# Attention stage of a four-layer graph network: row numbers of two steps in one load and one comparison, a ring of 18 steps for the gathered rows, the block's maximum in other forms

## The reference

```python
def _L3_gnn_ref(x, edge_index, edge_attr, W, w_att, bias):
    h = x @ W
    src, dst = (edge_index[0], edge_index[1])
    x_i = h[dst]
    x_j = h[src]
    wa = w_att[0]
    alpha = x_i @ wa[:c] + edge_attr @ wa[c:c + ce] + x_j @ wa[c + ce:]
    alpha = jnp.where(alpha > 0, alpha, NEG_SLOPE * alpha)      # 0.2
    m = jax.ops.segment_max(alpha, dst, num_segments=n)
    m = jnp.where(jnp.isfinite(m), m, 0.0)
    a = jnp.exp(alpha - m[dst])
    s = jax.ops.segment_sum(a, dst, num_segments=n)
    a = a / (s[dst] + 1e-16)
    out = jax.ops.segment_sum(a[:, None] * x_j, dst, num_segments=n) + bias
    return out
...
x = _layernorm(x + _L3_gnn_ref(x, edge_index, edge_attr_16, L3_gnn_W, L3_gnn_w_att, L3_gnn_bias), axis=-1)
```

## Time and profile before

| what | value |
|---|---|
| median of 3 runs | 3815.82 us (3812.74 to 3816.24) |
| profiled execution | 3803.94 us, span 3802.2 us |
| VectorE busy over the span | 3118.7 us (82%) |
| TensorE busy | 3011.9 us (79%) |
| ScalarE busy | 2164.2 us (57%) |
| GpSimd busy | 1355.7 us (36%) |
| HBM traffic | 237 GB/s over the span |
| attention stage | from about 2855 us to the end |

### The profile page before, as it was taken

How to read it: one execution, slowest core, us unless ns; L and a number is a source line. 1 busy time by engine, 2 the same in 40 slices (tenths; PEclk the granted TensorE clock), 3 DMA queues, 4 the chain that set the end, 5 groups by cost and what they waited for, 6 DMA issues and landing times.

```text
span 3802.2 us, 124955 instructions
## 1 busy us (share of the span) xinstructions
PE 3011.9 (79%) x50473; PEld 2686.6 (71%) x50473; DVE 3118.7 (82%) x6534; ACT 2164.2 (57%) x5758; POOL 1355.7 (36%) x1644
## 2 busy tenths in 40 slices
PE   0288888888888869999778777787776888888786
PEld 0177777777777759899677777777766777777775
DVE  7599999999999933223599999999977889888996
ACT  5323333333333320000388888888866888888887
POOL 2000000000000000000088887887883555555554
PEclk9999999999999989999899999999986878888887
DMA  8156666666666689898687777777747888888884
GB/s 216 55 157 207 207 208 208 209 210 209 207 210 208 214 284 380 344 339 323 232 269 239 253 250 242 250 256 232 247 157 248 265 260 272 269 270 260 270 270 141
DMA packets 655934, 907.61 MB, mean 239 GB/s; under 512 B 363977, under 2 KB 587882, under 8 KB 636411
## 3 DMA queue, kind: packets, MB, share of 16 engines
q1 hardware_dynamic: 633240, 800.64, 65.5%
q10 hardware_dynamic: 19763, 94.38, 6.5%
q0 software_dynamic: 2352, 4.52, 0.6%
HBM read 651.96 MB, written 247.40 MB: 237 GB/s over the span
## 4 chain that ended last, share of the span: by engine, by line
DVE 37%; PE 31%; DMA 9%; issue 8%; ACT 7%; SPq 2%; POOL 1%; ACTq 0%; DVEq 0%; POOLq 0%
PE ps L630 7%; PE ps L976 7%; DVE U L758 5%; DMA U<-AD 3%; DVE A L1292 3%; DVE EDG L781 3%; DVE EDG L1316 3%; DMA A<-ROWS 3%; DMA T<-ROWS 3%; DVE U L1284 3%; PE ps L1199 2%; DVE U L1666 2%; DVE EDG L1671 2%; ACT U L546 2%; PE ps L1211 2%
## 5 line engine op out<-in xcount | busy, mean ns | idle before, releaser
L546 ACT ACTIVATE U<-ps 128x512 bf16<-128x512 f32 (+1 forms) x637 | 359.1, 573 | 666.0 <-PE ps L642 664.5
L1169 POOL TENSOR_TENSOR EDG<-U,edge 128x256 f32<-128x256 f32 x343 | 244.1, 712 | 780.4 <-DVE edge L1312 678.6
L1491 ACT ACTIVATE U<-U,T 128x65 f32<-128x65 f32 x1806 | 459.7, 340 | 76.4 <-PE ps L1582 65.5
L491 POOL DMA_INDIRECT U<-REC,nod x49 | 45.0, 918 | 1163.5 <-PE ps L586 1042.5
L976 PE MATMUL ps<-U 128*128 128x192 bf16 x4802 | 416.9, 248 | 30.8 <-DMA U<-AD 30.5
L1199 PE MATMUL ps<-U 128*128 128x65 bf16 x7203 | 296.8, 198 | 173.4 <-DVE A L1292 171.5
L976 PEld LDWEIGHTS ps<-U 128*128 128x128 bf16 x4802 | 401.9, 98 | 39.3 <-DMA U<-AD 35.9
L781 DVE TENSOR_TENSOR EDG<-edge,EDG 128x896 bf16<-128x896 bf16 x686 | 407.8, 620 | 10.0 <-DMA OSD<-EDG 9.1
L1199 PEld LDWEIGHTS ps<-U 128*128 128x128 bf16 x7203 | 258.0, 100 | 195.8 <-DVE A L1292 191.0
L1519 POOL TENSOR_TENSOR U<-U 128x455 f32<-128x455 f32 x258 | 275.8, 1069 | 296.2 <-DVE U L1666 296.2
L655 PE MATMUL ps<-EDG,U 128*128 128x193 bf16 x2401 | 312.9, 252 | 62.3 <-ACT U L546 40.8
(11 more groups left out here) (299 smaller groups left out, 7148.5 us busy)
## 6 DMA issues: line engine op xcount, KB each, us to landing
U<-AD SPq DMA_DIRECT2D x98, 1568.0 KB, 8.5
U<-ROWS SPq DMA_DIRECT2D x343, 448.0 KB, 4.6
OND<-EDG SPq DMA_DIRECT2D x343, 224.0 KB, 2.3
OSD<-EDG SPq DMA_DIRECT2D x343, 224.0 KB, 3.1
AD<-U ACTq DMA_DIRECT2D x49, 1568.0 KB, 6.4
EDG<-ROWS SPq DMA_DIRECT2D x343, 224.0 KB, 5.0
U<-OND SPq DMA_DIRECT2D x303, 224.0 KB, 5.2
EDG<-OSD SPq DMA_DIRECT2D x189, 224.0 KB, 4.8
```

The costliest lines, as they stand in the source:

```text
L546: ev4.by(act.activation(prow[i % NPW][:, P * g:P * (g + m)], ps[4 + gg % 2][:, 0:P * m], ACT.Copy))
L1491: ins = act.activation(V4[k % NV][:, 0, c, :], H[d % 3][:, s, :], ACT.Copy, scale=a4[d % 2][:, s:s + 1])
```

## The change

Row numbers. ROWS3 is laid out with the source rows of all blocks first and the target rows after them, so that two steps stand next to each other also across blocks. `sources(u)` and `targets(u)` load the row numbers of steps 2u and 2u + 1 at once (448 KB, 128 x 1792), and VectorE compares them at once. There are NU4 = 172 such pairs in place of 343 steps, 5 slots of double size for each kind, in other places of SBUF. SyncE issues the sources of pair t // 2 + 4 at even t; VectorE compares the sources of pair t // 2 + 2 at even t, and the targets of pair u at t = 2u + 7. The targets of a pair are issued at t = 2u + 4, or later when TensorE has not yet reached L1572's place for the block whose steps occupied the slot (`freed`).

Ring. `H` is a ring of 18 steps, where it was 21 (three blocks). Where a block goes over the end of the ring, alpha and the setting of the column are made in two pieces. The preparation uses a view `Hp` of the last 7 steps' place on.

Maximum. The step that makes max(0.2 m, m) was a scalar_tensor_tensor with m as both inputs. It is now a tensor_scalar with m as input and as scalar, made twice: to SBUF, and to one column `top` of PSUM. The two remainders are taken from `top` and from a further PSUM column `rest`, which makes one more subtraction. The waits for VectorE's own results stay.

```diff
-        ROWS3 = dram("ROWS3", (NB, 2, NB * P), BF16)
+        ROWS3 = dram("ROWS3", (2, NB, NB * P), BF16)
...
-        NRL, NRW = 10, 6
-        drow = [EDG[:, NB * 98 + 448 * i:NB * 98 + 448 * (i + 1)].bitcast(BF16) for i in range(NRL)]
-        H = [part(NB * 65 * i, NB * 65).rearrange("p (b f) -> p b f", f=65) for i in range(3)]
+        NRL, NRW = 5, 5
+        drow2 = [EDG[:, NB * 98 + 896 * i:NB * 98 + 896 * (i + 1)].bitcast(BF16) for i in range(NRL)]
+        NHR = 18
+        H = [part(G * 65 * i, G * 65).rearrange("p (b f) -> p b f", f=65) for i in range(NHR)]
+        Hp = part(G * 65 * (NHR - G), NB * 65).rearrange("p (b f) -> p b f", f=65)
...
+        NU4 = (NG + 1) // 2
+        srcs, dsts = (ROWS3[f].rearrange("d e -> (d e)") for f in range(2))
...
+        top, rest = ps[3][:, 3 * P + 64:3 * P + 65], ps[3][:, 3 * P + 65:3 * P + 66]
...
         def pairs4_sp(sp):
-            def sources(k):
-                r = k % NRW
-                if k >= NRW:
-                    sp.wait_ge(hg.at, hg.o + k - NRW + 1)
-                slo_ld[r].by(sp.dma_start(srow[r], ROWS3[k // G, 0, 7 * P * (k % G):7 * P * (k % G + 1)].partition_broadcast(P)), 16)
-
-            def targets(k):
-                r = k % NRL
-                if k >= NRL:
-                    sp.wait_ge(alg.at, alg.o + (k - NRL) // G + 1)
-                dlo_ld[r].by(sp.dma_start(drow[r], ROWS3[k // G, 1, 7 * P * (k % G):7 * P * (k % G + 1)].partition_broadcast(P)), 16)
+            def sources(u):
+                r, n = u % NRW, cells(u)
+                if u >= NRW:
+                    sp.wait_ge(hg.at, hg.o + 2 * (u - NRW) + 2)
+                elif u == 4:
+                    sp.wait_ge(pre_d.at, G)
+                slo_ld[r].by(sp.dma_start(srow2[r][:, 0:n], srcs[2 * G * P * u:2 * G * P * u + n].partition_broadcast(P)), 16)
+
+            def targets(u):
+                r, n = u % NRL, cells(u)
+                if u >= NRL:
+                    sp.wait_ge(alg.at, alg.o + freed(u) + 1)
+                dlo_ld[r].by(sp.dma_start(drow2[r][:, 0:n], dsts[2 * G * P * u:2 * G * P * u + n].partition_broadcast(P)), 16)
+
+            def freed(u):
+
+                return (2 * (u - NRL) + 1) // G
...
             for t in range(LASTT):
-                if t + 5 < NT:
-                    sources(t + 5)
-                _, g, k = due4(t, 4)
-                if k is not None and g < 3:
-                    targets(k)
-                d = block4(t, 8)
-                if d is not None:
-                    for g in range(3, G):
-                        targets(G * d + g)
+                if t % 2 == 0 and t // 2 + 4 < NU4:
+                    sources(t // 2 + 4)
+                while nt < NU4 and t >= max(2 * nt + 4, G * freed(nt) + 15 if nt >= NRL else 0):
+                    targets(nt)
+                    nt += 1
...
         def pairs4_act(act):
...
-                    if k >= 3 * G:
-                        act.wait_ge(vok.at, vok.o + k - 3 * G + 1)
-                    elif k == 2 * G:
+                    if k >= NHR:
+                        act.wait_ge(vok.at, vok.o + k - NHR + 1)
+                    elif k == NHR - G:
                         act.wait_ge(pre_w.at, pre_w.o + G)
...
         def pairs4_dve(dve):
...
+            def sources(u):
+                r, n = u % NRW, cells(u)
+                dve.wait_ge(slo_ld[r].at, slo_ld[r].o + 16 * (u // NRW + 1))
+                ost.by(dve.tensor_scalar(srow2[r][:, 0:n], srow2[r][:, 0:n], iotap[:, 0:1], None, ALU.is_equal))
...
             for t in range(LASTT):
-                if t + 3 < NT:
-                    sources(t + 3)
+                if t % 2 == 0 and t // 2 + 2 < NU4:
+                    sources(t // 2 + 2)
...
+                _, _, k = due4(t, 7)
+                if k is not None and k % 2 == 0:
+                    targets(k // 2)
...
-                    zok.by(dve.tensor_tensor(z4[d % 2], H[d % 3][:, :, D], E3v[:, d, :, 3], ALU.add))
+                    for s0, h_ in parts:
+                        s1 = s0 + h_.shape[1]
+                        ins = dve.tensor_tensor(z4[d % 2][:, s0:s1], h_[:, :, D], E3v[:, d, s0:s1, 3], ALU.add)
+                    zok.by(ins)
...
-                    dvf.by(dve.scalar_tensor_tensor(RIf[:, d, 3:4], m4[:, 1:2], 0.2, m4[:, 1:2], ALU.mult, ALU.max))
+                    dvf.by(dve.tensor_scalar(RIf[:, d, 3:4], m4[:, 1:2], 0.2, m4[:, 1:2], ALU.mult, ALU.max))
+                    dvf.by(dve.tensor_scalar(top, m4[:, 1:2], 0.2, m4[:, 1:2], ALU.mult, ALU.max))
                     own()
-                    dvf.by(dve.tensor_tensor(RIf[:, d, 4:5], RIf[:, d, 3:4], RI[:, d, 3:4], ALU.subtract))
+                    dvf.by(dve.tensor_tensor(RIf[:, d, 4:5], top, RI[:, d, 3:4], ALU.subtract))
+                    dvf.by(dve.tensor_tensor(rest, top, RI[:, d, 3:4], ALU.subtract))
                     own()
-                    miok.by(dve.tensor_tensor(RIf[:, d, 5:6], RIf[:, d, 4:5], RI[:, d, 4:5], ALU.subtract))
+                    miok.by(dve.tensor_tensor(RIf[:, d, 5:6], rest, RI[:, d, 4:5], ALU.subtract))
```

More of the change, by code:

```diff
@@ L1392, in gnn_kernel @@
         dlo_ld = [on(hot_st[i], 32 * len(range(i, NB * NH7, NHB))) for i in range(2)] \
[L1393 removed]
+            + [on(ar_ld[i], 32 * len(range(i, NB, NA))) for i in range(NA)]
+        tail_ld = [sem(f"tail_ld{i}") for i in range(5)]
         def due4(t, off):
@@ L2083, in gnn_kernel @@
         s66v = S66[0:EP, :].rearrange("(p k) f -> p k f", p=P)
-        g_ld = [again(dlo_ld[5 + i]) for i in range(NRT)]
+        g_ld = [again(tail_ld[i]) for i in range(NRT)]
         s_st = [sem(f"s_st{i}") for i in range(NRT)]
```

66 lines of the change are left out of this document (35 added, 31 removed).

## The result

The changed kernel takes 3778.23 us in the median of four runs (3774.54 to 3782.79), the kernel before beside it 3816.03 us (3812.74 to 3820.24). The ratio is 0.9899, with a 95% interval of 0.9886 to 0.9913: 38 us faster. The forecast was 3753 us, 63 us faster; the time lies in its range of 3705 to 3800, and within 3 us of rival 1's 3781.

The account below looks back on a forecast made before the run. No engine plainly bound the attention stage; VectorE was busiest (88%). Terms took VectorE's path from 18.23 to 15.8 us a block; the other engines made it 16.93, saving 62 us over 48 blocks: 3753 us, range 3705 to 3800.

Parts of the forecast that it names:

- rival 1: VectorE in attention: waits for GpSimd stay or reappear in the next L1666; 35 us saved, 3781 us; chance 0.24.
- comparisons: VectorE, per block: seven comparisons of 1792 columns replace 14 of 896, saving 1.3 us (1.1 to 1.7).
- wait for source rows: VectorE's DMA wait: sources loaded four steps ahead instead of two arrive in time, saving 1.03 us a block.
- wait for target rows: VectorE's target comparison: one pair in seven is loaded one step ahead, costing 0.3 us a block (0 to 1.15).
- maximum: VectorE's block maximum: five short operations replace three of 1.32 us, saving 0.5 us, or losing 0.3 if held.
- ring, alpha in two pieces: VectorE's L1675 and L1677 at the ring's wrap: 0.3 us in 16 of 49 blocks, 0.1 us a block.
- GpSimd gets as many openings as before: VectorE and GpSimd in attention: argument against waits for GpSimd staying or reappearing in the next L1666; no size given.
- Rival 2: Late target pair in attention: landing over 9 us makes the kernel slower; at 10 us, 3843 us; chance 0.07.
- That costs nothing: Ring of 18 steps: slot reuse waits for a ScalarE step ahead on ScalarE itself, claimed to cost nothing.
- The others' floor: Attention block: ScalarE near 15.7 us and DMA 15.9 end after VectorE's 15.8, giving a period of 16.93 us.
- mixture term: Attention period from what engines together reach: 16.7 us for five blocks in seven, 17.5 for two, 16.93 us.
- the chain through all engines: ScalarE over VectorE, GpSimd, TensorE and back sets the pace; sign: VectorE waits over 2 us a block for ScalarE.

Follow-up runs that it names:

- e5: Kernel before, with GpSimd's remainder made for one of the seven cells only: 3773.9 us, ratio 0.9900.
- e6: Changed kernel, with GpSimd's remainder made for one of the seven cells only: 3724.1 us, ratio 0.9759.
- e8: Changed kernel with a sixth slot for target pairs and a ring of 16 steps instead of 18: 3798.1 us, ratio 0.9957.
- e9: Changed kernel with only the ring shortened, 16 steps instead of 18: 3800.0 us, ratio 0.9948.
- e2: Kernel before with the new five-operation maximum alone: 3799.6 us, ratio 0.9958.
- e1: Changed kernel with the block's maximum in its former three operations: 3783.2 us, ratio 0.9913.
- e7: Changed kernel with VectorE's target comparison ahead of the remainder L1688 instead of behind it: 3781.0 us, ratio 0.9914.
- e12: Changed kernel with the exponential, ScalarE's products, both remainders, the sum and the OND loads one step later: 3768.9 us, ratio 0.9884.
- e11: Changed kernel with GpSimd's remainder made for four of the seven cells: 3741.3 us, ratio 0.9788.

## Why the forecast was right in direction and too large by 25 us

| term, us a block | forecast | measured |
|---|---|---|
| comparisons | −1.3 (−1.1 to −1.7) | −0.41 |
| wait for source rows | −1.03 | −1.03 (none left in the window) |
| wait for target rows | +0.3 (0 to 1.15) | +0.20 in the window, +0.40 over the stage |
| maximum | −0.5 (to +0.3) | −0.43 (1.32 to 0.90) |
| ring, alpha in two pieces | +0.1 | −0.3 |
| remainder L1666, L1688 | 0 | +0.27 (4.71 to 4.98) |
| L1725 and L1751 | 0 | +0.22 |
| VectorE's wait for ScalarE | not in its path | +0.46 |
| period | −1.30 | −0.55 |

**The comparison term is the one that failed.** The step took "1.3, nearer the mean" of L1284, 0.818 us, for a form that here has means of 0.83 to 0.95. The median was right (0.68, forecast 0.73). L1284 stands beside other work of GpSimd than L1631 and L1636 do. L1284's mean stands for 7 × 0.086 = 0.6 us a block of waiting; here it is 1.60, and 0.89 of them are the 21 target comparisons of 2.77 us, which meet L1532 and two remainders in a row. e5 and e6 show the term at 1.51 without the collisions. "GpSimd gets as many openings as before" was the reason given against rival 1. The runs bear it out and refute what was drawn from it: GpSimd works on as many cells and finds as many openings, and so the waiting stayed and moved.

**Durations were added as if they stood end to end.** The busy terms of the table sum to −0.41 − 0.43 − 0.3 + 0.27 + 0.22 = −0.65 us a block, while VectorE's busy time in the window fell by 0.21. Records of neighbouring operations overlap: in the timeline above L1741 starts 0.08 us before L1740's record ends, the comparison 0.08 before L1743's. A block has 37.2 records in the window after (1473 / 39.6) and 41.8 before (1606 / 38.4); 4.6 fewer at 0.09 us are 0.41 that no one saves. The traces agree when the windows' records are added up: the sum of all VectorE durations fell from 18.57 to 17.96 us a block, what they overlap from 2.27 to 1.87. A 1792 comparison therefore replaces two that cost less than two records of 0.448.

**Source rows: right.** The 39.6 us in the window are gone; one wait of 3.1 us is left in the stage. **Target rows: right in size**, though in 11 long waits (19.4 us), not up to 25 of a microsecond; the landing took 3.3 to 9.8 us, median 6.0. Rival 2's 9 us are inside that spread, but it concerns one load in many. e8 beside e9 shows that to be rid of these waits gains nothing here, since others take the time.

**The maximum: the size was right** (−0.43), the reason only in part. L1737, from SBUF to SBUF, takes 0.211 to 0.217 us. In after only 6 of the 49 meet L1532, so the better test is e2, at the place where the old form stood: there the new form (L1710) begins 31 times while GpSimd is in the last of its flag operations, and never lasts over 0.216 us, while L1709 in the kernel before was held in all 24 such cases. The Trainium skill says in VectorE: DVE Perf Modes (Mode 2×_2P) that a scalar form from SBUF to SBUF can use both read ports, and the forecast took from it that this form might wait; no such wait shows in a form of one element. On 1792 bf16 columns a form with the same kinds of operands does wait. Where the wait had gone, though, later long operations paid, as rival 1's second half says (it named the next L1666; in e2 they were alpha and the source comparisons): on top of the rest the maximum is worth 0.14% only, alone 0.42%. And by e1 the old form, too, takes just 0.92 us in the changed kernel, so there hardly any of the −0.43 is the new form's doing.

**The ring: wrong sign, small.** Alpha fell to about 0.32 us a block from a mean of 0.60, by waiting less, which says nothing of the ring. What the ring can cost showed in e9: shortened by two more steps it costs 22 us. "That costs nothing" holds at 18 and not at 16.

**The others' floor: too low, for the wrong reason.** The forecast added a mixture term to VectorE's 15.8 and came to 16.93. VectorE's path without its waits for ScalarE is 17.675 − 0.79 = 16.9, the very number of rival 1, and the period 17.7 for its 17.5. That the numbers meet is partly luck: rival 1 let the comparisons save 1.05 us and the maximum lose 0.3, and they measured −0.41 and −0.43. DMA wasn't near a bound: the share fell to 0.84 where 0.92 was expected, since larger transfers moved more bytes with less of the engines' time. VectorE's waits for ScalarE are 0.79 us a block, far from the 2 us at which the forecast called the chain through all engines the pace. Yet e7, the sixth slot and e12 each removed a wait of 8 to 41 us in 700 and got 0 to 0.15% for it: with VectorE busy 91%, ScalarE 89% and waits for each other both ways, a wait that goes is mostly a wait elsewhere. Only shortening GpSimd's operation (e5, e6, e11) moved the time much.

**What stays open.** Whether TensorE's granted clock has a part in the gain (0.85 of full speed in the window before, 0.88 after; but e9 has 0.88 at a period of 18.13 and e5 0.88 at 17.49, so it doesn't set the period alone); whether the maximum and the merging are worth anything on top of the rest (0.14% and 0.15%, neither outside its interval); and whether e12 is truly faster than after.

## What to carry to other kernels

Price a longer VectorE operation by its median and add its waits for GpSimd separately, by what GpSimd starts beside it in that place, not by the mean of the same form in another stage. Where one engine is held by a busy neighbour, as VectorE was by GpSimd here, taking the wait out of one operation may only move it into the next long one; shortening the neighbour's operation removed it. Look for the few longest operations of a group before putting its mean down to all of them: 21 of 172 held more than half of the comparisons' waiting. Where a wait for a slot is against the engine's own work, keep the last use more than a step away.

## What the runs showed of the hardware that was not expected

- GpSimd gets in at the boundary of two VectorE operations, then holds the second if it is a long one on SBUF: a comparison of 1792 columns took 1.37 us instead of 0.68 behind another one that took 0.68 beside the waiting GpSimd, and two of 896 in a row 1.50 instead of 0.90. One VectorE operation can be held by several of GpSimd in a row: 2.77 us instead of 0.68, over the end of L1532 and two remainders.
- A scalar form on one element, SBUF to SBUF, wasn't held (0.217 us at most; in e2 it met the last flag operation 31 times); operations of one element with two SBUF operands were (24 of 24 such cases of L1709, and a subtraction up to 1.38 us).
- An ACTIVATE that waits for the one right ahead on ScalarE starts 0.10 us after its end instead of 0.10 before.
- Four cells of seven in GpSimd's remainder already give 1.1% of the 1.4% that one cell gives.
- Transfers of 448 KB in place of 224 moved 274 GB/s at a DMA share of 0.84, where it was 268 at 0.87.
